# Attention and expert kernel on one core: part of a store sent ahead, one first-choice step moved up, attention outputs turned at other steps

## The reference

```python
x = x + 0.5 * ffn(layernorm(x), gate_weight, gate_up_proj, down_proj)
x = x + attention(layernorm(x))
x = x + 0.5 * ffn(layernorm(x), gate_weight, gate_up_proj, down_proj)

# attention: 16 heads of 8 features, and 32 rotary features that all heads share
scores = einsum('bqhd,bkhd->bhqk', q, k) + einsum('bqr,bkr->bqk', q_rope, k_rope)[:, None]
w = softmax(where(causal, -inf, scores / scale)); out = einsum('bhqk,bkhd->bqhd', w, v) @ W_o
# experts: a token's place in an expert's list is the count of earlier tokens with that expert
pos = (cumsum(onehot) * onehot).sum(-1) - 1
```

## Time and profile before

| | us |
|---|---|
| median of 3 runs | 550.43 (548.26 to 551.25) |
| the profiled execution, its own time | 550.67 |
| its span | 549.0 |
| TensorE busy | 517.1 |
| VectorE busy | 420.2 |
| ScalarE busy | 256.3 |
| GpSimd busy | 98.1 |

### The profile page before, as it was taken

One profiled execution on the slowest core, in us unless ns is written; L12 is line 12 of the kernel. 1 busy time (PEld: TensorE's weight loads), 2 busy tenths in 40 slices (PEclk: granted clock), 3 DMA queues, 4 the chain that ended last, 5 costly groups with the idle time before them and its releaser, 6 DMA issues.

```text
span 549.0 us, 11100 instructions
## 1 busy us (share of the span) xinstructions
PE 517.1 (94%) x3534; PEld 330.4 (60%) x3559; DVE 420.2 (77%) x1425; ACT 256.3 (47%) x430; POOL 98.1 (18%) x215
## 2 busy tenths in 40 slices
PE   5988999989799899999999999999999987999996
PEld 2856677774356456565565555556544644676775
DVE  5786888885889677778788777878831898798875
ACT  1574222244533456666565666656577641222212
POOL 2120000002593103021221203122131130000000
PEclk8799999999999899999999999999999998999999
DMA  9895300000045001010000101000000180000002
GB/s 181 138 251 199 77 2 2 2 2 3 1 153 184 29 21 41 2 51 9 31 30 22 38 3 53 7 32 29 0 2 1 38 223 2 1 2 2 1 3 77
DMA packets 25095, 26.71 MB, mean 49 GB/s; under 512 B 6704, under 2 KB 18576, under 8 KB 25040
## 3 DMA queue, kind: packets, MB, share of 16 engines
q1 hardware_dynamic: 23024, 23.54, 16.1%
q10 hardware_dynamic: 2016, 2.46, 1.3%
HBM read 17.04 MB, written 8.78 MB: 47 GB/s over the span
## 4 chain that ended last, share of the span: by engine, by line
PE 81%; DVE 8%; DMA 4%; ACT 3%; issue 2%; SPq 1%; ACTq 0%; DVEq 0%
PE ps L1651 14%; PE ps L1740 13%; PE ps L1677 13%; PE ps L1342 11%; PE ps L1430 7%; PE ps L1445 5%; PE ps L1459 3%; PE ps L1647 2%; PE ps L1264 2%; PE ps L1333 2%; PE ps L1706 2%; DVE xn L857 2%; DMA kn_d<-nl 1%; DMA x<-in_L_attn_x 1%; PE ps L1582 1%
## 5 line engine op out<-in xcount | busy, mean ns | idle before, releaser
L767 ACT ACTIVATE probs<-ps 128x1024 f32<-128x1024 f32 (+3 forms) x192 | 146.1, 812 | 96.8 <-PE ps L1677 96.6
L1185 DVE TENSOR_REDUCE mxh<-ps 128x1 f32<-128x512 f32 (+2 forms) x176 | 114.8, 687 | 29.1 <-PE ps L1651 28.5
L1651 PE MATMUL ps<-Kst,Qst 120*128 120x512 f32 (+3 forms) x384 | 129.2, 402 | 3.9 <-DMA Qst<-qn_d 2.6
L1677 PE MATMUL ps<-Qst,Kst 121*128 121x512 f32 (+3 forms) x384 | 94.4, 351 | 0.8 <-ACT probs L767 0.7
L1651 PEld LDWEIGHTS ps<-Kst,Qst 120*128 120x128 f32 x384 | 66.2, 191 | 46.1 <-DVE mxh L1185 17.3
L515 POOL TENSOR_SCALAR_AFFINE_SELECT probs<-probs 128x256 f32<-128x256 f32 x128 | 51.5, 408 | 199.8 <-ACT probs L767 198.5
L1182 DVE CUSTOM_DVE_ANT_0 summed<-ps,maskf 128x384 f32<-128x384 f32 (+1 forms) x128 | 74.3, 618 | 13.5 <-PE ps L1651 13.5
L1740 PE MATMUL ps<-probs,Vst 128*32 128x512 f32 (+3 forms) x768 | 81.8, 499 | 0.1
L1677 PEld LDWEIGHTS ps<-Qst,Kst 121*128 121x128 f32 x384 | 67.2, 191 | 15.1 <-ACT probs L767 5.7
L1342 PE MATMUL ps<-onehot,xp 128*128 128x512 bf16 (+1 forms) x250 | 65.9, 385 | 4.5 <-DVE onehot L936 2.6
L936 DVE TENSOR_SCALAR onehot<-iotab,posm 128x128 bf16<-128x128 bf16 (+1 forms) x352 | 60.4, 250 | 0.2
(11 more groups left out here) (179 smaller groups left out, 622.7 us busy)
## 6 DMA issues: line engine op xcount, KB each, us to landing
wgn<-in_L_ffn_gate_up_proj SPq DMA_DIRECT2D x8, 384.0 KB, 6.4
guT_d<-gus SPq DMA_DIRECT2D x6, 384.0 KB, 5.2
gus<-guT_d SPq DMA_DIRECT2D x6, 384.0 KB, 6.1
Kst<-kn_d SPq DMA_DIRECT2D x28, 64.0 KB
Qst<-qn_d SPq DMA_DIRECT2D x28, 64.0 KB
wdn<-in_L_ffn_down_proj SPq DMA_DIRECT2D x8, 192.0 KB, 7.6
dnT_d<-dns SPq DMA_DIRECT2D x6, 192.0 KB, 5.9
dns<-dnT_d SPq DMA_DIRECT2D x6, 192.0 KB, 7.2
```

The source lines that it names most:

```text
L767: e.activation(probs[n % RING][:, 2 * b:2 * b + 2, lo:BANK], ps[:, 2 * b:2 * b + 2, lo:BANK], ACT.Exp, scale=SCALE).then_inc(probs_ready, 1)
L1185: e.tensor_reduce(to, s.rearrange("p (q k) -> p q k", k=w), AX.X, ALU.max).then_inc(mx_ready, 1)
L1651: ins = e.matmul(ps[:, bank, i * w:(i + 1) * w], Qst[p][h][0:ROWS, column(b, jt * P):column(b, jt * P) + P], Kst[p][h][0:ROWS, column(b, o ...
L1677: ins = e.matmul(ps[:, 2 * b + h, lo:BANK], Kst[p][h][0:ROWS + 1, column(b, kt * P):column(b, kt * P) + P], Qst[p][h][0:ROWS + 1, column(b ...
```

## The change

It has three parts. The stores of pieces 4 to 7 from ScalarE's queue carry rows 16 to 31 alone (`SECOND`); rows 32 to 127 follow from SP's queue behind `stage_shift(0, 0, 1)`, with a wait for their landing ahead of the loop over pairs. Rows 0 to 15 of these pieces are no longer stored. In the opening there are 18 products of zeros for 12, and `positions(0, 3)`, with two products of zeros ahead of it, stands before `turn_weights(3)`. And `OLDOUT` goes from step 1 to 2, `EARLYTURN` from 3 to 5, `NEWOUT` from 5 to 8 (it stays at 5 in the last pair).

```diff
-LATETURN, OLDOUT, EARLYTURN, NEWOUT = 0, 1, 3, CLOSES[0] + 2
+LATETURN, OLDOUT, EARLYTURN, NEWOUT = 0, 2, 5, 8
+SECOND = slice(2 * HD, 4 * HD)
-        def store_nope(e, u):
+        def store_nope(e, u, rows, landed):
-                e.dma_start(dst[r, :, piece(c)], raw(src[:, :])).then_inc(nope_stored[u], 16)
+                e.dma_start(dst[r, rows, piece(c)], raw(src[rows, :])).then_inc(landed, 16)
@@ SyncE
-                        store_nope(e, u)
+                        store_nope(e, u, slice(0, P), nope_stored[u])
             stage_shift(0, 0, 1)
+            for u in range(NC, 2 * NC):
+                store_nope(e, u, slice(SECOND.stop, P), rest_stored)
+            e.wait_ge(rest_stored, 32 * NC)
             ring_loop(e, pair_step, 0, NPAIR - RING - 1)
@@ ScalarE
-                    store_nope(e, NC + 2 * g)
-                    store_nope(e, NC + 2 * g + 1)
+                    for u in (NC + 2 * g, NC + 2 * g + 1):
+                        store_nope(e, u, SECOND, nope_stored[u])
@@ TensorE
-            idle_work(7, 12)
+            idle_work(7, 18)
             positions(0, 2)
+            idle_work(1, 2)
+            positions(0, 3)
             turn_weights(3)
-            positions(0, 3)
             turn_weights(4)
@@
-                    if n == NEWOUT:
+                    if n == (CLOSES[0] + 2 if last else NEWOUT):
```

More of the change, by code:

```diff
@@ L315, in build @@
         nope_stored = [sem(f"nope_stored{u}") for u in range(2 * NC)]
+        rest_stored = sem("rest_stored")
         low_done, lowh_ready, lowl_ready, asm_done, asm_act, asm_dve = (
```

## The result

The changed kernel took 542.36 us in the median of 4 executions (540.56 to 546.73), the kernel before 549.63 beside it (548.26 to 551.25), a ratio of 0.988 with an interval of 0.985 to 0.991. The profiled execution is another matter. It was the slowest of the four, 546.73 us with a span of 545.0, 0.7 us from the forecast. So two things have to be explained: where the 3.94 us between the two profiled spans went, and why the other executions are up to 6.2 us faster than the profiled one.

What follows compares the result with a forecast made beforehand. TensorE was taken as the bound, with 81% of the chain. Stores less late loads (4.3 - 0.9 = 3.4), opening 0.6 and turns 0.7 give 4.7 us off the profiled 550.67: 546.0, range 543.0 to 549.0.

Steps and rivals of the forecast that it cites:

- The stores' gain: Pair 0: with small early stores the second group of loads no longer waits for a store, gaining 4.3 us.
- The first group of loads: Pair 1's unit 0: `EARLYTURN` at 5 delays SP's loads by 5.0 us, so TensorE waits, losing 0.9 us.
- much later: Rival at pair 1's unit 0: first loads need the full 12.4 us, losing 4.6 us; time 549.7, chance 0.22.
- The opening and the turns: Opening: moved positions remove TensorE's wait, gain 0.6 us; loop: `OLDOUT` at 2 gains 0.12 us a pair, 0.7 together.
- the zeros' term in the sum: Opening: six more zeros delay the gate's transpose by 0.5 us, which is covered, so cost 0.
- the clock stays up in the opening: Rival in the opening: the clock does not fall, work from 14.43 to 20.30 takes 2.9 us less; 543.1, chance 0.12.
- the last sentence of the sum: The profiled execution is 0.24 us above the median of 550.43, inside the runs' spread of 3 us, so left uncorrected.

Runs made afterwards that it cites:

- stores_alone: The kernel before with only the stores' rows divided into early and late ones; zeros, positions and turns as before: 546.03 us, ratio 0.992.
- turns_alone: The kernel before with only `OLDOUT`, `EARLYTURN` and `NEWOUT` moved to 2, 5 and 8, the large stores kept: 549.62 us, ratio 0.999.
- early_at_3: The changed kernel with `EARLYTURN` back at step 3 instead of 5: 542.23 us, ratio 0.987.
- z18_alone: The kernel before with only the products of zeros at the start raised from 12 to 18: 548.28 us, ratio 0.997.
- last_old_at_1: The changed kernel with the old output turned at step 1 instead of 2 in the last pair only: 542.06 us.
- pos_alone: The kernel before with only `positions(0, 3)` and its two products of zeros moved ahead of `turn_weights(3)`: 548.53 us, ratio 0.999.

## Why the prediction was right, and where it was wrong

**The stores' gain: right.** 4.3 us were forecast for pair 0 and 4.32 measured, and stores_alone brings 3.7 in the median by itself.

**The first group of loads: right in mechanism, too dear.** The term was a loss of 0.9 us. The forecast wait stands in seven of nine profiles, 0.59 to 1.10 us long, and the loads were in place 8.7 to 9.3 us after their first issue, 8.7 forecast. But TensorE can have a wait for VectorE there instead (0.72 us in the change's first profile), so it cost 0 to 0.4 us, and 1.4 in the one profile in which the clock fell behind it. The change's first profile has none of it: SP's first load came at 167.32 and not at 168.6, and when VectorE let the unit start, 8.85 us later, it was in place. Of the rival "much later", turns_alone shows that it needs the large stores.

**The opening and the turns: right, a little small.** 0.86 us for 0.6, and about 0.16 us a pair for 0.12, 0.95 for 0.7 in all. `EARLYTURN` at 5, taken at nothing, costs 0.07 us a pair beside early_at_3.

**The hit on the profiled execution is luck.** 546.0 was forecast and 546.73 measured, but the terms won 6.1 us (4.32, 0.86 and 0.95) where 4.7 were forecast, and 2.2 us went that no term had: 0.29 and 0.38 ahead of the first pair, and 1.5 from pair 7 on. Of the last, 0.46 us come from the place of a few instructions in SP's program. About 1 us is the late fall of the clock in the last experts, which half of all profiles have.

**The step that failed** is the zeros' term in the sum, "Cost 0", with nothing beside it for the clock, and the chance of 0.12 that went with it for "the clock stays up in the opening". With it fell the last sentence of the sum, that the profiled execution stands for the median. The runs split the change in medians. With 12 zeros it brings 5.0 us (549.55 to 544.55), near the sum's 4.7. The six zeros more, put at nothing, bring another 1.7 (to 542.85), and 1.4 in the kernel before (z18_alone). At least seven of the changed kernel's ten executions had the fast opening, six by their mean clock and one by its profile, and there the rival's price was about right: 3.15 us up to the first one-hot product for 2.9.

The argument against that rival does not hold. It was that a second idle time, after 10.6 us, was untouched by the zeros. In the kernel before the clock fell before that idle time began, as busy time by stretch shows:

```profile
7.00:10.40 3.40, 1.39 (x7) 0.44 (x5) 1.54 (x9) 0.28 (x2) 1.01 (x3) 1.00 1.20 209
10.50:13.80 3.30, 1.98 (x8) 1.15 (x7) 3.19 (x18) 0.92 (x4) 0.53 (x1) 0.50 1.25 179
```

And in the profiles of early_at_3 and last_old_at_1 the clock survived both idle times, 1.09 and 1.19 us. What makes the clock fall in one execution and not in the next stays open; what is shown is how often it does with each number of zeros, in the few executions there are. The profiled execution of before had the slow kind of opening, and so had four other profiles with 12 zeros; in pos_alone's the fall was short and cost little.

## What to carry to other kernels

Before a forecast is set against a median, see whether the executions agree on the clock: here 0.01 of mean clock was 4 us, more than half of what the change brought. Where one profile shows the clock low in a stretch in which TensorE is the bound, forecast both cases, and give the fast one more than a token chance if the change adds work ahead of it. When a forecast meets the profiled execution, add up the terms one by one all the same: here two errors of over 1 us had cancelled. A transfer that is late behind a large store is worth dividing the store for. A step that puts off the issues of another queue should be tried with and without that: with the large stores the turns alone bought nothing, since one wait of 2.64 us gave way to another of 3.76.

## What the runs showed of the hardware

- Two executions with the same instructions in the opening and the same idle times in TensorE's list (1.08 and 1.18 us, 1.09 and 1.19) had the granted clock at 0.5 from 14.4 to 21.2 us in one (the change) and at 1.00 in the other (early_at_3). From the second turn to the first one-hot product this is 21.12 us for 17.97.
- The number of zero products at the start shifts how often the clock stays up: a mean clock of 0.997 or more in 1 of 16 executions with 12, in 6 of 10 with 18. Why is open.
- A fall of the clock costs by where it lands. Those that began between 445 and 455 us, ahead of or beside VectorE's tables, cost nothing that shows; those between 456 and 466, of the same 3.4 us, about 1.3 (ten profiles at 139.8 to 140.3 us for the last stretch, ten at 138.4 to 138.9).
- Two DMA issues of SP that follow each other stand 0.68 us apart or 1.02, by where they lie in SP's program: 0.68 in the five profiles without the divided stores, 1.02 in all with them but the two with the repeated waits (four instructions more), where it is 0.68 again. On the path this cost 0.46 us.
- Eight loads, four of 64 KB and four of 32, were in place 8.7 to 9.3 us after the first issue with small stores beside them.
